# A mixture-of-experts stage that sorts its rows by expert through DRAM, in place of multiplying every row by all eight experts

## What is computed

```python
x = x + _L0_ffn_ref(_layernorm(x, axis=-1), ...)
logits = jnp.einsum('bsd,ed->bse', x, router_w) + router_b
probs = jax.nn.softmax(logits, axis=-1)
weights = jnp.max(probs, axis=-1)
top1 = jnp.argmax(probs, axis=-1)
y_all = jnp.einsum('bsd,eod->bseo', x, expert_w) + expert_b
y = jnp.take_along_axis(y_all, top1[:, :, None, None], axis=2)[:, :, 0, :]
out = y * weights[:, :, None]
```

## Time and profile before

| | us |
|---|---|
| median of 3 runs | 3716.37 |
| lowest, highest | 3715.56, 3717.41 |
| span of the profiled execution | 3715.1 |
| PE busy in the profiled execution | 3532.5 (95%) |
| DVE busy | 2509.9 (68%) |
| ACT busy | 1524.9 (41%) |
| POOL busy | 1672.3 (45%) |

### The profile page before, as it was taken

One profiled execution on the slowest core, in us unless ns is written; L12 is line 12 of the kernel. 1 busy time (PEld: TensorE's weight loads), 2 busy tenths in 40 slices (PEclk: granted clock), 3 DMA queues, 4 the chain that ended last, 5 costly groups with the idle time before them and its releaser, 6 DMA issues. The chain is left out here.

```text
span 3715.1 us, 59691 instructions
## 1 busy us (share of the span) xinstructions
PE 3532.5 (95%) x21448; PEld 2521.2 (68%) x21448; DVE 2509.9 (68%) x5415; ACT 1524.9 (41%) x3014; POOL 1672.3 (45%) x2143
## 2 busy tenths in 40 slices
PE   7888888888999999999999998999989999999999
PEld 5666766666555888888887665666656556666555
DVE  8999999998666555555554445777743367777332
ACT  5878777874001222222222224555521145555211
POOL 6888888986000000000001225777721157777221
PEclk9999999998999999999999999999999999999999
DMA  1000000001210100001001211112111111121121
GB/s 42 1 12 12 12 12 4 10 7 42 75 34 20 41 12 11 11 13 35 10 13 56 68 65 58 41 35 61 35 62 51 37 58 35 41 69 33 49 74 34
DMA packets 150763, 129.35 MB, mean 35 GB/s; under 512 B 20852, under 2 KB 147592, under 8 KB 150472
## 3 DMA queue, kind: packets, MB, share of 16 engines
q1 hardware_dynamic: 150472, 125.54, 10.9%
HBM read 87.73 MB, written 37.77 MB: 34 GB/s over the span
## 5 line engine op out<-in xcount | busy, mean ns | idle before, releaser
L2909 ACT ACTIVATE win_probs<-win_sc,win_nbias,tile_rn 128x256 f32<-128x256 f32 x512 | 282.3, 561 | 313.3 <-DVE win_nbias L2993 313.3
L420 POOL TENSOR_TENSOR ssm_acc<-ssm_acc,ssm_weighted 128x512 f32<-128x512 f32 x255 | 337.9, 1333 | 103.8 <-ACT ssm_weighted L565 103.1
L406 POOL TENSOR_SCALAR ssm_ub<-ssm_uT,ssm_bcT 128x512 f32<-128x512 f32 x512 | 357.7, 718 | 25.8 <-PE ssm_pu L1107 21.9
L1107 PEld LDWEIGHTS ssm_pu<-ident,ssm_ub 128*128 128x128 f32 x2048 | 241.5, 144 | 181.4 <-issue 87.5
L3095 PE MATMUL win_pa<-win_w_wqkv,tile_hT 128*128 128x512 f32 x744 | 362.5, 624 | 0.0
L1107 PE MATMUL ssm_pu<-ident,ssm_ub 128*128 128x128 f32 x2048 | 312.8, 282 | 48.2 <-DVE ssm_state L780 32.1
L1123 PE MATMUL ssm_pt<-ident,ssm_state 128*128 128x128 f32 x2040 | 280.5, 280 | 48.3 <-DVE ssm_acc L790 30.4
L2512 PE MATMUL glu_up<-block_hT,glu_w_w 128*128 128x512 f32 x704 | 308.9, 597 | 7.7 <-DVEq L82 7.7
L780 DVE TENSOR_TENSOR_SCAN ssm_state<-ssm_da,ssm_carry,ssm_pu 128x512 f32<-128x512 f32 x256 | 312.6, 1262 | 3.1 <-ACT ssm_da L553 3.0
L1822 POOL TENSOR_TENSOR lin_rstd<-lin_mv,lin_eps 128x1 f32<-128x1 f32 x30 | 5.7, 190 | 670.0 <-DVE lin_mv L168 670.0
L780 DVE TENSOR_TENSOR_SCAN ssm_state<-ssm_da,ssm_pu 128x512 f32<-128x512 f32 x256 | 296.9, 1201 | 5.4 <-PE ssm_pu L1107 2.7
(11 more groups left out here) (372 smaller groups left out, 7659.7 us busy)
## 6 DMA issues: line engine op xcount, KB each, us to landing
x<-block_y SPq DMA_DIRECT2D x16, 512.0 KB, 2.9
block_add<-x SPq DMA_DIRECT2D x16, 512.0 KB, 5.8
tile_raw<-in_tables SPq DMA_DIRECT2D x64, 128.0 KB, 2.2
a<-tile_y SPq DMA_DIRECT2D x64, 128.0 KB, 1.7
block_xs<-a SPq DMA_DIRECT2D x32, 256.0 KB, 3.3
block_x<-a SPq DMA_DIRECT2D x16, 512.0 KB, 5.3
x<-block_half_y SPq DMA_DIRECT2D x16, 256.0 KB, 2.1
block_x<-x SPq DMA_DIRECT2D x8, 512.0 KB, 3.9
```

Of the source, the lines that this page charges most:

```text
L406: nc.gpsimd.tensor_scalar(ub[:, i % 2, t, :], uT[:, k % 2, t, :], bcT[:, k % 2, t, n:n + 1], 1.0, ALU.mult, ALU.mult).then_inc(ub_ready.se ...
L420: nc.gpsimd.tensor_tensor(acc[:, k % 2, t, :], acc[:, k % 2, t, :], weighted[:, j, :], ALU.add)\
L1107: last = nc.tensor.transpose(pu[c][:, t * P:(t + 1) * P], ub[:, i % 2, t, c * P:(c + 1) * P], ident)
L2909: nc.scalar.activation(probs[:, head, :], sc[j][:, r, :], ACT.Exp, bias=nbias[:, g, j, r:r + 1], scale=rn[:, turn.side, 0, head:head + 1], ...
```

## The change

The rows are brought to their experts. The stage now has two parts.

In the first, all 8 blocks are normalised and routed as before. In addition PE computes, with a triangular matrix and a matrix of ones, the rank of every row among the rows of its expert (`rank`); POOL adds up the counts (`count`); DVE turns ranks into row numbers (`positions`); and POOL writes the rows to `sorted_rows` in DRAM by four indirect DMAs per block (`scatter`), one of 128 rows each. A row carries 4 further numbers: its gain, the reciprocal root of its variance, its shift and its token number, 1040 bytes in all. Each expert has room for all 4096 rows there.

Ten small DVE steps (`table`) then give, for each of 39 tiles of 128 rows of one expert (32 and up to 7 more, since an expert's last tile may be part full), the first row and the column of the expert's weights. In the second part SP gathers a tile, ACT normalises it, PE transposes it, ACT copies it, PE multiplies it by one expert, DVE adds bias and product, and POOL writes the 128 rows to their places by an indirect DMA. SP, PE and DVE each load a number of the table into a register per tile (`value_load`) and address by it. Rows that hold no token go to rows of their own ahead of x2.

The opening work of linear attention follows the last tile, save `fold`, which precedes the first. The state-space stage clears `sorted_rows` (33792 rows) by 8 DMAs, two near its start and one after each of its first six blocks.

```diff
 E = 8
+CAP = T
+EXTRA = NT + E - 1
+ROW = D + 4
+GAIN, RSTD, SHIFT, TOKEN = D, D + 1, D + 2, D + 3
+SORTED = 384 * 88
...
+            lines = sorted_rows.rearrange("(c p r) d -> p c (r d)", p=P, r=3)
+            zeros = following.zeros[:, 0:3 * ROW].unsqueeze(1).to_broadcast([P, 11, 3 * ROW])
+
+            def clear_rows(j):
+                sp.dma_start(lines[:, j * 11:(j + 1) * 11, :], zeros).then_inc(rows_cleared, 16)
+
+            clear_rows(6)
+            clear_rows(7)
 
...
+                if k < 6:
+                    clear_rows(k)
                 if k == N - 2:
                     sp.wait_ge(zeros_sent, 16 * len(padded))
+                    sp.wait_ge(rows_cleared, 16 * 8)
+                    sp.wait_ge(dt_ready.sem, dt_ready.at(N - 1))
                     sp.wait_ge(z_made.sem, z_made.at(N - 1))
...
+        sp.dma_start(self.m.experts, w["experts"].rearrange("(k p) n -> p k n", p=P)).then_inc(self.experts_in, 16)
+        sp.dma_start(self.m.expert_b[:, :], w["expert_b"].partition_broadcast(P)).then_inc(self.experts_in, 16)
...
+    def shifts(self, dve, k):
+        nc = self.nc
+        dve.wait_ge(self.rstd_ready.sem, self.rstd_ready.at(k))
+        if k == 0:
+            dve.wait_ge(self.loaded, 16 * 5)
+        nc.vector.scalar_tensor_tensor(self.column(k, SHIFT), self.mv[:, k % 2, :, 0], -1.0, self.column(k, RSTD),
+                                       ALU.mult, ALU.mult).then_inc(self.shift_ready.sem, 1)
+        nc.vector.tensor_copy(self.column(k, TOKEN).bitcast(mybir.dt.int32), self.tokens[:, k * TB:(k + 1) * TB])
...
+    def rank(self, pe, k, bank):
+        nc, hot = self.nc, self.hot[:, k % 2, :, :]
+        if k >= 1:
+            pe.wait_ge(self.counted.sem, self.counted.at(k - 1))
+        if k >= 2:
...
+            nc.tensor.matmul(tiles, self.ones, self.counts[:, t * E:(t + 1) * E].unsqueeze(1).to_broadcast([P, TB, E]),
+                             start=(t == 0), stop=False, skip_group_check=True)
+        pe.wait_ge(self.steps.sem, self.steps.at(k, 6))
+        nc.tensor.matmul(tiles, self.earlier, hot, start=False, stop=False, skip_group_check=True)
+        for back in range(1, TB):
+            last = nc.tensor.matmul(tiles[:, back:TB, :], self.ones, hot[:, 0:TB - back, :], start=False, stop=(back == TB - 1),
+                                    skip_group_check=True)
+        last.then_inc(self.ranked.sem, 1)
+
...
+    def count(self, pool, k):
+        pool.wait_ge(self.steps.sem, self.steps.at(k, 6))
+        pool.wait_ge(self.ranked.sem, self.ranked.at(k))
+        self.nc.gpsimd.tensor_tensor(self.counts, self.counts, self.hot[:, k % 2, :, :].rearrange("p t e -> p (t e)"),
+                                     ALU.add).then_inc(self.counted.sem, 1)
+
+    def positions(self, dve, k, bank):
+        nc = self.nc
+        ranks = bank[:, 0:TB * E].rearrange("p (t e) -> p t e", e=E)
+        dve.wait_ge(self.ranked.sem, self.ranked.at(k))
+        if k:
+            dve.wait_ge(self.placed.sem, self.placed.at(k - 1))
+        nc.vector.tensor_tensor(self.hits[:, :, :], ranks, self.hot[:, k % 2, :, :], ALU.mult).then_inc(self.hits_ready.sem, 1)
+        dve.wait_ge(self.hits_ready.sem, self.hits_ready.at(k))
+        with nc.allow_low_precision(reason="one whole number below 2**16 and zeros"):
+            nc.vector.tensor_reduce(self.place[:, k * TB:(k + 1) * TB], self.hits[:, :, :], AX.X, ALU.add)\
+              .then_inc(self.placed.sem, 1)
+
...
+            for k in range(2, 6):
+                own.load_block(sp, k)
             for sem, total in pending:
                 sp.wait_ge(sem, total)
...
+            for k in (6, 7):
+                sp.wait_ge(scattered[k - 6], 16 * TB)
+                own.load_block(sp, k)
+            sp.wait_ge(table_steps.sem, table_steps.at(0))
+            for j in range(3):
+                sp.wait_ge(scattered[j], 16 * TB * (1, 1, NBLK - 2)[j])
+            for j in range(EXTRA):
+                at = sp.value_load(start_row[0:1, j:j + 1], min_val=0, max_val=SORTED - P)
+                if j >= SLOTS:
+                    sp.wait_ge(y_out[j % SLOTS], sent(j - SLOTS))
+                sp.dma_start(tile_rows(j), sorted_rows[bass.ds(at, P), :]).then_inc(rows_in[j % SLOTS], 16)
+            for j in range(EXTRA - SLOTS, EXTRA):
+                sp.wait_ge(y_out[j % SLOTS], sent(j))
             following.load(sp)
...
+            def scatter(k):
+                rows = own.rows(k)
+                pool.wait_ge(own.placed.sem, own.placed.at(k))
+                for t in range(TB):
+                    at = k * TB + t
+                    nc.gpsimd.indirect_dma_start(sorted_rows[:, :], bass.IndirectOffsetOnAxis(own.place[:, at:at + 1], 0),
+                                                 rows[:, t, :], None).then_inc(scattered[min(k, 2)], 16)
 
             following.constants(pool)
+            own.factors(pool, 1)
+            own.count(pool, 0)
+            own.factors(pool, 2)
+            scatter(0)
+            for k in range(1, NBLK):
+                if k + 2 < NBLK:
+                    own.factors(pool, k + 2)
+                own.count(pool, k)
+                scatter(k)
+            for j in range(EXTRA):
+                pool.wait_ge(summed.sem, summed.at(j))
+                nc.gpsimd.indirect_dma_start(dst[:, :], bass.IndirectOffsetOnAxis(target[:, j:j + 1], 0),
+                                             m.tiles_y[:, j % SLOTS, :], None).then_inc(y_out[j % SLOTS], 16)
...
+            def bias(j):
+                rows, at = tile_rows(j), dve.value_load(columns[0:1, j:j + 1], min_val=0, max_val=(E - 1) * D)
+                dve.wait_ge(rows_in[j % SLOTS], sent(j))
+                if j >= SLOTS:
+                    dve.wait_ge(y_out[j % SLOTS], sent(j - SLOTS))
+                nc.vector.tensor_tensor(target[:, j:j + 1], rows[:, TOKEN:TOKEN + 1].bitcast(mybir.dt.int32),
+                                        own.tokens[:, NT + j:NT + j + 1], ALU.max)
+                nc.vector.scalar_tensor_tensor(m.tiles_y[:, j % SLOTS, :], m.expert_b[:, bass.ds(at, D)], rows[:, GAIN:GAIN + 1],
+                                               rows[:, 0:D], ALU.mult, ALU.add).then_inc(biased.sem, 1)
+
+            def total(j):
+                y = m.tiles_y[:, j % SLOTS, :]
+                dve.wait_ge(biased.sem, biased.at(j))
+                dve.wait_ge(tile_made.sem, tile_made.at(j))
+                nc.vector.scalar_tensor_tensor(y, ex[j % BANKS][:, 0:D], tile_rows(j)[:, GAIN:GAIN + 1], y, ALU.mult, ALU.add)\
+                  .then_inc(summed.sem, 1)
+
+            own.statistics(dve, 1)
+            own.statistics(dve, 2)
+            own.shifts(dve, 1)
+            own.shifts(dve, 2)
+            for k in range(1, NBLK):
+                if k + 2 < NBLK:
+                    own.statistics(dve, k + 2)
+                own.choose(dve, k, logit_banks[k % 2])
+                if k + 2 < NBLK:
+                    own.shifts(dve, k + 2)
+                own.positions(dve, k, rank_banks[k % 2])
+            following.lay_projection(dve)
+            table()
+            dve.wait_ge(own.experts_in, 16 * 2)
+            bias(0)
+            for j in range(EXTRA):
+                if j + 1 < EXTRA:
+                    bias(j + 1)
+                total(j)
+            following.statistics(dve, 0)
+            following.normal(dve, 0)
+            following.hidden(dve, small)
+            following.features(dve, tp)
+            following.statistics(dve, 1)
+            following.normal(dve, 1)
...
+            def transposes(j):
+                pe.wait_ge(tile_n.sem, tile_n.at(j))
+                if j >= 2:
+                    pe.wait_ge(tile_hT.sem, tile_hT.at(j - 2))
                 for k in range(KD):
+                    last = nc.tensor.transpose(tp[j % 2][:, k * P:(k + 1) * P], m.n[:, j % AHEAD, k * P:(k + 1) * P], ident)
+                last.then_inc(tile_tp.sem, 1)
+
+            def product(j):
+                at, hidden = pe.value_load(columns[0:1, j:j + 1], min_val=0, max_val=(E - 1) * D), tile_hidden(j)
+                pe.wait_ge(tile_hT.sem, tile_hT.at(j))
+                if j >= BANKS:
+                    pe.wait_ge(summed.sem, summed.at(j - BANKS))
+                for k in range(KD):
+                    last = nc.tensor.matmul(ex[j % BANKS][:, 0:D], hidden[:, k, :], m.experts[:, k, bass.ds(at, D)],
+                                            start=(k == 0), stop=(k == KD - 1))
+                last.then_inc(tile_made.sem, 1)
...
+            own.transposes(pe, 1, tp)
+            own.route(pe, 1, logit_banks[1])
+            own.transposes(pe, 2, tp)
+            own.route(pe, 2, logit_banks[0])
+            for k in range(1, NBLK):
+                own.rank(pe, k, rank_banks[k % 2])
+                if k + 2 < NBLK:
+                    own.transposes(pe, k + 2, tp)
+                    own.route(pe, k + 2, logit_banks[k % 2])
+            add_up()
+            following.fold(pe, tp)
```

(10 more changed lines are left out.)

529 lines of the change are left out of this document (249 added, 280 removed).

## The result

The changed kernel takes 3610.6 us (median of 4 runs, 3608.2 to 3611.9) against 3716.0 us before (median of 4, 3710.6 to 3717.4): a ratio of 0.972, 95% interval 0.971 to 0.973. The forecast was 3632 us in a range of 3573 to 3700. The saving was forecast at 83.9 us; the medians give 105.4, the profiled executions 105.0 (3715.1 to 3610.1).

A forecast was written before the change was run, and what follows sets the result against it. PE's own work, mostly expert products, was taken to bound the stage. The next stage's start, 997.4 + 29c + 38r = 1129.2 us against 1213.1, gave 3716.4 - 83.9 = 3632.5 us, range 3573 to 3700.

The forecast's parts named there:

- The mechanism: Whole stage: PE's own work sets the pace; expert products take 220 us, seven eighths of it for zero gates.
- c: What one scatter (indirect DMA of 128 rows) costs POOL, in both parts: 1.4 us, range 1.0 to 2.0.
- r: Pitch per tile in the second part: 2.4 us, range 1.9 to 2.7, with PE filled at 1.2 GHz.
- The first part: Routing all rows: POOL sets the pace, block 1's row numbers at about 951 us, end at 999 us.
- The turn: From last scatter to first tile: 8 us, with the fold hidden by a margin of some 2 us.
- The second part: 39 tiles at pitch r, 38r in the sum; PE half idle at full clock, so falling to half clock.
- rival 1: Second part: register loads hide, clock stays up, r = 1.3 us; 130.7 us less, 3586 us; chance 0.22.
- The tail: After the last tile: 24.4 + c us, 2.5 us of it the last gap, plus 5 us for half clock.
- The clock's price: In the tail: some 11 us of PE work after a pause, 5 us more for the half clock.
- Rivals 2 and 3: POOL's scatter costs 2.5 us, 3680 us, chance 0.18; or over 3.05 us, 3747 us at 3.5, chance 0.07.
- Rival 4: State-space stage: clears or bigger loads aren't hidden; any late one holds it 24 us or more; chance 0.03.

The follow-up runs named there:

- e1: Changed kernel with unused filler matmuls on PE in the first part, 14 ahead and three at two places per block: 3595.7 us, ratio 0.968.
- e2: Changed kernel with each scatter of both parts issued a second time, into spare DRAM: 3683.3 us.
- e6: Changed kernel with the fold moved behind the last tile and this stage's semaphores not cleared at its end: 3625.0 us.
- e3: Changed kernel with constant start rows, weight columns and target rows in the second part, so no register loads: 3614.3 us.
- e4: Changed kernel with the second part's 39 tiles stored by plain POOL DMAs to fixed rows, not indirect ones: 3610.6 us.
- e7: Changed kernel with PE filler up to block 4, fold groups spread over blocks 3 to 7, filler at turn and tail: 3611.6 us, ratio 0.973.
- e10: Changed kernel with e1's filler, 24 filler matmuls in the tail and a POOL drain behind tile 0's factors: 3601.7 us, ratio 0.970.
- e5: Changed kernel with 20 filler matmuls behind the last tile and a POOL drain right after its last scatter: 3621.1 us.
- e8: The changed kernel itself, unaltered, run again on another chip: 3625.4 us.

## Why the prediction was right, point by point

*The mechanism* was right where the gain comes from: PE's own products bounded the stage, and one expert a tile takes off most of them. *The range* held, but that the time came within 22 us of 3632.5 is luck: two terms were off by 20 and 42 us, with opposite signs. With the measured c and r the forecast's own sum gives 997.4 + 36.8 + 48.9 = 1083.1 us, 27 us before the measured 1110.5. I had said of the clock "What moves r up from 1.3 is the clock", for the second part, and priced the first at full clock. It was the other way round.

*The first part*: block 1's row numbers at 957.4 us (forecast 951), the last scatter at 1016.9 (999). Two things made it. I let POOL set the pace at 7.7 us a block (5.9 for blocks 6 and 7), while PE at half clock needed 9.97 (e1, e2). And for block 1 I left out that PE's transposes and router of block 2 stand ahead of rank(1), all at half clock (e1's filler brings these row numbers 5.6 us sooner).

*The price c* was right: 1.27 us for 1.4, in both parts. With e2's doubling it is also shown where it matters: in the second part throughout, in the first only behind the last block.

*The turn*: 10.7 us for 8. The fold was not hidden with a margin of 2 us: ACT came to the first gathered tile at 1024.3 us, 1.7 us after its rows were in. e6 doesn't settle what moving it gives (0.2 to 1.6 us), since its products also hold the clock up.

*The second part*, r: 1.286 us for 2.4, rival 1's value. It carried the largest error, 42.3 us. The register loads cost 0.10 to 0.20 us a tile, hidden behind POOL (e3, e4), and the clock was at 1.00. The Trainium skill, page "TensorE: Matmul & The Clock Gate", section "HAM oscillation — how this bites in real kernels", by which I expected the half clock in both parts, gives the first part's clock (0.50 for 80 us) and not the second's (1.00). Its mechanism isn't what the first part's rows show either: the page has long waits for data between the products, and here PE is busy 44 of 50 us and waits 1.18 us once a block. (The rival that goes with a full clock is rival 1; the prediction calls it the second there.) I had written that PE would be half idle at full clock. By my own numbers that was wrong: 1.12 us of work against POOL's 1.4 us, the largest of the others, is 80%; measured, 1.08 us of PE's work (e3) in 1.286 is 84%. It is the first part that would be half idle at full clock: PE's 8.8 us a block at half clock are an estimated 4.4 at full, of 9.97.

*The tail*: 34.0 us for 30.8. The clock's price was there, but about half of the 5 us I had put on it (10.29 us for 7.66, back at 7.74 with filler in e7 and e10). What was missing is POOL's drain, some 5.4 us in the stage's last gap, which I had put at the 2.5 us of before.

The terms in one line: the first total at 1027.6 us in place of 1007.2, +20.4; tiles -42.3, tail +3.2; 1129.2 - 18.7 = 1110.5 us. Rivals 2 and 3 fell with c = 1.27 us. The Trainium skill, page "SBUF — State Buffer", section "A bandwidth-pool intuition that's wrong (but worth ruling out)", has a GpSimd DMA at some 3100 ns beside a VectorE copy. No such copy runs in the second part, so its case isn't tested; beside DVE's other instructions, busy 20 of 25 us, a scatter held POOL 960 ns. Rival 4 fell: the stage before ended at 932.5 us, and between 928.9 and 935.3 in the twelve experiments, against 934.7 before: the clears hide, to within the 3 us either way by which this varies.

## What to carry to other kernels

When a change turns long products into many short ones, price TensorE's time at half clock until a row says otherwise, and look for where its idle time is: filler into a free bank bought 12 us there, and too much of it gave the gain back. A stage's pitch is the largest of the engines' own times, so ask how full the slowest is at that pitch before assuming its clock falls. Doubling one engine's work shows its slack in one run, and a last gap that grows without a row in it is worth a drain at an earlier, idle place.

## What the runs showed of the hardware

- After POOL has issued DMAs, its first drain held it for 6.0 us (e5). It isn't the wait for the last of them to land: without that drain the long gap stands 25 us behind the last scatter's issue (1077.84, then 1103.17 to 1110.53). The kernel before, whose POOL issues none in this stage, has no such gap. The gap is the same with 32 indirect and 39 plain (e4) as with 71 indirect, 7.4 us, and 7.9 us with 142 (e2).
- The granted clock stayed at 0.50 for some 80 us (933 to 1015), with PE busy 44 of the 50 us from 950 to 1000 with products of 8 to 128 columns, and rose within three tiles of 256-column products (e6).
- The same program has a second part of 48.9 us in one profile and 60.4 in another (e8), while the medians of the kernel before agree on all chips within 0.1%. Chip and moment aren't told apart: all seven runs on the second and third chip have the long tiles, none on the first and fourth. A comparison across chips needs the unaltered kernel beside it.
